# Key, value and gate products of two batches as three fp32r products each, with the norm's affine folded into the weights

## The chip, the cores and the metric

The kernel runs on 1 core of one Trainium2 chip. The metric is device microseconds of one execution, and the number quoted for a kernel is the median of its runs. TensorE is PE, its weight loads PEld, VectorE DVE, ScalarE ACT, GpSimd POOL and SyncE SP.

## The reference, cut to what matters

Four batches (B=4) of T=1024 tokens with D=128 features go through two time-mixing layers, a layer norm, a mixture of eight experts (top 2, hidden width 512) and a last norm. One time-mixing layer is

```python
normed = _layer_norm(x, ln_w, ln_b)            # (x - mu) * rsqrt(var + EPS) * w + b
k = einsum('btd,ed->bte', normed, Wk)
v = einsum('btd,ed->bte', normed, Wv)
r = sigmoid(einsum('btd,ed->bte', normed, Wr))
state = 0.95 * state + 0.05 * (k * v)           # a scan over the tokens
y = einsum('btd,ed->bte', r * state, Wo);  return x + y
```

and an expert computes `silu((x Wfc + bfc) * (x Wgate + bgate)) Wproj + bproj`.

## The kernel before

**Order of the work.** A head does the time mixing of batches 0 and 1 and the routing of batch 0. Then come four periods, one for each batch b, in which the experts of batch b run. A period has 32 points (8 experts times 4 blocks of 128 hidden units). Beside the experts of batch b, period b also routes batch b+1 and mixes batch b+2; the batches 2 and 3 are therefore mixed inside the periods 0 and 1. The order of each engine is written out by hand in tables that say what follows which point: TENSOR_MIX, SCALAR_MIX, VECTOR_MIX and POOL_MIX for the mixing of batch b+2 (lines 106 to 135). Every engine works through its own list in order and waits on semaphores.

**A point.** PE multiplies the gathered tokens by a gate block and an fc block (`hidden_pair`, lines 760 to 780): each is three fp32r matmuls of 308 columns, high part by high part, low by high and high by low. ACT copies the gate product out and adds its bias (`gate_copy`, line 984, tile gate_s), DVE multiplies (`product`, line 1299, tile prod), ACT takes silu of two blocks at a time (`silu`, line 991, tile hidden), PE projects (`project`, line 795) after the points 2 and 3 of the next expert, and DVE copies the result out (`copy_out`, line 1311) at the first point of an expert. `hidden_pair` of a point waits for the product of two points before.

**Mixing of batch 2 or 3.** It goes by halves of 512 tokens, n = 0 and 1 for the first layer, n = 2 and 3 for the second. For one half: DVE norms (`norm_of`, line 1095; it waits for POOL's rstd), PE transposes the four tiles into bank[0] (`turn`, line 619, after points 9, 12, 18 and 21), ACT copies bank[0] out with ln_w as scale and ln_b as bias (`turned`, line 912, tile normT), and PE multiplies (`kvr`, lines 639, 649 and 651, after points 10, 13, 20 and 22): k into bank[1], v into bank[2], r into bank[0], each one fp32 matmul of 512 columns, which the records show as two. ACT copies k (`k_of`, line 929) and takes tanh of r (`r_of`, line 939). DVE multiplies k and v (line 1112), scans (1122) and forms r times the state (1127): `mix`, after points 11, 14, 21 and 23. PE multiplies by Wo (`out`, line 679), DVE adds to x (line 1147) and takes the statistics of the next norm (lines 1070 and 1076).

**DVE's list around the halves** (VECTOR_MIX): norm(1) stands after the product of point 9, norm(3) after that of point 19, mix(0), mix(1), mix(2), mix(3) after those of 11, 14, 21 and 23. The copy_out of an expert stands ahead of the products of points 12, 20 and 24, skip_sum (line 1103) after that of point 20.

**Head.** Its lists are TENSOR_HEAD to POOL_HEAD (lines 67 to 99). The last entries of DVE are stats(2,0), stats(2,1) and slots(0,0) to slots(0,2); the last three form the low parts of the first gathered tokens (line 1161), for which the first expert waits.

Of the kernel before, what the change touches and what calls it, by code (L numbers as in the profile page):

```python
# [36 lines left out]
P = 128  # L37
# [32 lines left out]
               ("logits", 0, 0), ("logits", 0, 1), ("turn", 1, 0), ("turn", 1, 1), ("count", 0, 0),  # L70
               ("kvr", 1, 0), ("kvr", 1, 1), ("carry", 1, 0), ("out", 1, 0), ("carry", 1, 1), ("out", 1, 1),
               ("turn", 1, 2), ("turn", 1, 3), ("kvr", 1, 2), ("kvr", 1, 3), ("carry", 1, 2), ("out", 1, 2),
# [19 lines left out]
               ("scan", 1, 3), ("low", 6, 0), ("low", 6, 1), ("stats", 1, 4), ("stats", 1, 5), ("low", 7, 0),  # L92
               ("low", 7, 1), ("stats", 2, 0), ("stats", 2, 1), ("slots", 0, 0), ("slots", 0, 1),
               ("slots", 0, 2)]
# [17 lines left out]
SCALAR_ROUTE = {2: [("turned", 4)], 4: [("turned", 5)], 6: [("lead", 0)]}  # L112
VECTOR_MIX = {6: [("norm", 0)], 9: [("norm", 1)], 11: [("mix", 0)], 14: [("mix", 1)], 15: [("add", 0), ("stats", 2)],
              16: [("norm", 2)], 17: [("add", 1)], 18: [("stats", 3)], 19: [("norm", 3)], 20: [("skip_sum", 0)],
              21: [("mix", 2)], 23: [("mix", 3)], 24: [("add", 2)], 25: [("stats", 4)], 27: [("add", 3)],
              28: [("stats", 5)]}
# [89 lines left out]
def time_mix_moe(nc, h, ln_w, ln_b, Wk, Wv, Wr, Wo, router_w, router_b, w_fc, b_fc, w_gate, b_gate,  # L206
                 w_proj, b_proj, out):
    with ExitStack() as ctx:
        def sb(name, shape, dt=F32):
            return ctx.enter_context(nc.sbuf_tensor(name, shape, dt))  # L210
# [377 lines left out]
        def _(pe):  # L588
# [33 lines left out]
            def kvr(b, n):  # L622
                half = slice(HALF * (n % 2), HALF * (n % 2) + HALF)
                layer = n // 2
                c = step(b, n)
                between = banks_between(b)
                ps_r, ps_k, ps_v = mix_banks(b, n)
                if c > between:
                    pe.wait_ge(k_copied, c - between)
                fill("kvr", b, n, ps_k)  # L630
                if c == 1:
                    pe.wait_ge(weights_copied, 2)
                pe.wait_ge(turned_sb[0], c)
# [11 lines left out]
                if n == 2 and b >= 2:  # L645
                    pe.wait_ge(x_added, step(b, 1))
                if n == 0 and b >= 2:
                    pe.wait_ge(logits_copied, nth(b - 1, 2, 2))
                nc.tensor.matmul(ps_v[:, :], w_mix[:, L + layer, :], normT[:, half], start=True, stop=True)\  # L649
                  .then_inc(v_made, 1)  # L650
                nc.tensor.matmul(ps_r[:, :], w_mix[:, 2 * L + layer, :], normT[:, half], start=True, stop=True)\  # L651
                  .then_inc(r_made, 1)

            def carry(b, n):
# [73 lines left out]

            stages = {"turn": turn, "kvr": kvr, "out": out, "logits": logits, "count": count, "carry": carry}

# [29 lines left out]
            def hidden_pair(b, e, j):  # L760

                c = e * HC + j
                cols = slice(e * SLOTS, e * SLOTS + COLS)
                chunk = slice(P * j, P * j + P)
                if j == 0:
                    pe.wait_ge(slots_copied, nth(b, GROUPS, (e * SLOTS + COLS - 1) // (4 * P) + 1))
                if c == 0 and not later(b):
                    for read in (r_copied, k_copied, kv_made):
                        pe.wait_ge(read, nth(1, 4, 4))
                    pe.wait_ge(rows_made, 1)  # L770
                    pe.wait_ge(pool_low_made, 2 * LOW_BY_POOL)
# [124 lines left out]
        def _(act):  # L896
            def turned(b, n):
# [12 lines left out]
                tokens = slice(HALF * half, HALF * half + HALF)  # L910
                if not last:
                    nc.scalar.activation(normT[:, tokens], mix_banks(b, n)[0][:, :], ACT.Identity,
# [7 lines left out]
            def k_of(b, n):  # L920
# [6 lines left out]
                if c > 2 and n % 2 == 0:  # L927
                    act.wait_ge(state_made, c - 1)
                nc.scalar.activation(kv_sb[:, half], mix_banks(b, n)[1][:, :], ACT.Copy, scale=(1.0 - DECAY) / 2)\
                  .then_inc(k_copied, 1)  # L930

            def r_of(b, n):
# [4 lines left out]
                if c > 2:  # L937
                    act.wait_ge(out_made, c - 2)
                nc.scalar.activation(mixed[:, half], mix_banks(b, n)[0][:, :], ACT.Tanh, scale=0.5)\
                  .then_inc(r_copied, 1)  # L940

# [45 lines left out]
            def silu(b, e, i):  # L987
                act.wait_ge(prod_made, nth(b, POINTS, e * HC + 2 * i + 2))
                if e >= 2 or later(b):
                    act.wait_ge(o_made, nth(b, E, e - 1))  # L990
                nc.scalar.activation(hidden[:, e % 2, 2 * i:2 * i + 2, 0:COLS], prod[:, e % 2, 2 * i:2 * i + 2, :],  # L991
                                     ACT.Silu).then_inc(hidden_made, 1)

# [58 lines left out]
        def _(dve):  # L1052
# [53 lines left out]
            def kv_of(b, n):  # L1106
# [103 lines left out]
            def rows(b, _):  # L1210
# [28 lines left out]
                if b == LAST:  # L1239
# [4 lines left out]
            stages = {"stats": stats_of, "norm": norm_of, "kv": kv_of, "scan": scan_of, "mix": mix, "skip_sum": skip_sum, "add": add, "top": top,  # L1244
                      "choice": choice, "rows": rows, "slots": slots_low, "low": low_of}

# [46 lines left out]
            def product(b, e, j):  # L1293
# [3 lines left out]
                if j == 0 and (e >= 2 or later(b)):  # L1297
                    dve.wait_ge(hidden_made, nth(b, 2 * E, 2 * e - 2))
                nc.vector.scalar_tensor_tensor(prod[:, e % 2, j, :], pair[c % 2][1][:, 0:COLS], bfc_sb[:, e, j:j + 1],  # L1299
                                               gate_s[:, c % 2, :], ALU.add, ALU.mult).then_inc(prod_made, 1)  # L1300
# [361 lines left out]
```

## Time and profile before

| what | value |
|---|---|
| median of 3 runs | 366.13 us |
| lowest, highest run | 363.21 us, 367.05 us |
| span of the profiled execution, first to last instruction | 382.6 us |
| PE busy | 332.7 us, 87% of the span |
| DVE busy | 262.8 us, 69% |
| ACT, POOL busy | 166.2 us (43%), 203.9 us (53%) |

For the profiled execution the page gives the span and no other time of its own; what lies around the span is not stated. It is 16.5 us longer than the median of the runs. A matmul's record lasts longer than its turn on the engine, because matmuls are pipelined: what it costs PE is the distance from its start to the start of the next. The same holds, by less, for DVE and ACT. In the views PE's chain of waits is given in turns and the timeline in records.

### The profile page before, as it was taken

Reading aid. Unit: us, or ns where it says so; the run is one execution under the profiler, and the core shown is the slowest. Engines: PE = TensorE matmul, PEld = TensorE weight load, DVE = VectorE, ACT = ScalarE, POOL = GpSimd, SP = SyncE. Lnnn points to the kernel's source line nnn. Section 1 sums busy time; section 2 is a strip of 40 time slices with the busy share of each in tenths; the row PEclk is TensorE's granted clock in tenths of the full one; section 3 lists DMA queues with packets and bytes.
Section 4 is the critical chain, followed back from the end, with each engine's and each line's share of the span. In section 5 each row is a group of like instructions: output and inputs, shape, how many; then the busy total and the mean of one; then the engine's idle time right before and its main releaser. Section 6 shows DMA issues by size and latency. Waiting matters only on the chain.

```text
span 382.6 us, 7195 instructions
## 1 busy us (share of the span) xinstructions
PE 332.7 (87%) x2338; PEld 292.0 (76%) x2338; DVE 262.8 (69%) x853; ACT 166.2 (43%) x302; POOL 203.9 (53%) x244
## 2 busy tenths in 40 slices
PE   6889975869999999999999999877799986997880
PEld 3555653669879789997888999877689886987870
DVE  6688895787668868787787798831437684675225
ACT  2644434436545445555454445432435443363200
POOL 4185078850345642244557668377554437764752
PEclk9999896969999999999999999996999999898996
DMA  8949743150131133111114532222256111111152
GB/s 207 207 58 203 186 147 119 59 140 2 32 100 36 50 87 99 35 48 33 38 37 174 150 100 54 61 75 62 61 138 121 37 42 51 23 47 40 28 153 69
DMA packets 61246, 32.61 MB, mean 85 GB/s; under 512 B 15995, under 2 KB 58823, under 8 KB 61210
## 3 DMA queue, kind: packets, MB, share of 16 engines
q1 hardware_dynamic: 55322, 23.43, 25.3%
q0 software_dynamic: 4256, 7.94, 7.2%
q10 hardware_dynamic: 1632, 0.79, 0.7%
q8 instruction: 19, 0.31, 0.3%
q14 instruction: 17, 0.14, 0.1%
HBM read 19.01 MB, written 13.69 MB: 85 GB/s over the span
## 4 chain that ended last, share of the span: by engine, by line
PE 67%; issue 9%; DVE 8%; POOL 7%; another core or an unknown queue 3%; DMA 3%; ACT 3%; POOLq 0%; DVEq 0%; ACTq 0%
PE ps_o L795 20%; POOL slot_rows L1495 3%; PE pair0g L780 3%; PE pair0g L778 3%; PE pair1g L778 3%; PE bank L756 3%; PE bank L639 2%; PE pair1g L780 2%; PE bank L649 2%; PE pair0g L779 2%; PE bank L619 2%; PE pair1g L779 2%; PE bank L651 2%; PE pair1h L778 2%
## 5 line engine op out<-in xcount | busy, mean ns | idle before, releaser
L795 PE MATMUL ps_o<-proj_sb,hidden 128*104 128x128 f32 x768 | 99.7, 279 | 4.2 <-DVE o_sb L1311 2.1
L795 PEld LDWEIGHTS ps_o<-proj_sb,hidden 128*104 128x104 f32 x768 | 93.3, 175 | 5.8 <-issue 5.4
L1495 POOL DMA_INDIRECT slot_rows<-x_rows,row_to x64 | 72.5, 1133 | 45.1 <-DVE prod L1299 25.8
L1547 POOL DMA_INDIRECT picked<-expert_rows,row_from x48 | 49.9, 1039 | 37.4 <-DVE prod L1299 24.3
L984 ACT ACTIVATE gate_s<-pair0g,bgate_sb 128x308 f32<-128x308 f32 x64 | 33.1, 517 | 81.8 <-PE pair0g L780 52.7
L1299 DVE SCALAR_TENSOR_TENSOR prod<-pair1h,bfc_sb,gate_s 128x308 f32<-128x308 f32 x64 | 34.0, 532 | 32.3 <-ACT gate_s L984 17.7
L1299 DVE SCALAR_TENSOR_TENSOR prod<-pair0h,bfc_sb,gate_s 128x308 f32<-128x308 f32 x64 | 34.2, 534 | 26.4 <-ACT gate_s L984 11.8
L991 ACT ACTIVATE hidden<-prod 128x616 f32<-128x616 f32 x64 | 45.6, 712 | 7.7 <-DVE prod L1299 7.7
L984 ACT ACTIVATE gate_s<-pair1g,bgate_sb 128x308 f32<-128x308 f32 x64 | 33.0, 515 | 33.8 <-PE pair1g L780 22.2
L778 PE MATMUL pair1g<-slotT_hi,gate_hi 128*128 128x308 f32 x64 | 26.6, 416 | 10.0 <-DVE prod L1299 4.9
L1512 POOL DMA_INDIRECT returned<-o_sb,home x21 | 21.6, 1029 | 17.3 <-DVE prod L1299 11.2
L778 PE MATMUL pair0g<-slotT_hi,gate_hi 128*128 128x308 f32 x64 | 26.2, 409 | 4.0 <-DVE prod L1299 3.9
L1471 POOL TENSOR_TENSOR rstd<-shifted,power 128x4 f32<-128x4 f32 x24 | 26.2, 1093 | 2.0
L1311 DVE TENSOR_TENSOR o_sb<-ps_o,bproj_sb 104x384 f32<-104x384 f32 x32 | 17.5, 547 | 11.7 <-PE ps_o L795 7.4
L778 PEld LDWEIGHTS pair1g<-slotT_hi,gate_hi 128*128 128x128 f32 x64 | 12.4, 194 | 13.5 <-DVE prod L1299 6.7
L1467 POOL TENSOR_SCALAR shifted<-moments 128x4 f32<-128x4 f32 x24 | 6.8, 283 | 29.3 <-DVE moments L1076 29.1
L1161 DVE TENSOR_TENSOR slotT_lo<-bank,slotT_hi 128x512 fp32r<-128x512 f32 x20 | 13.8, 690 | 9.8 <-ACT slotT_hi L968 9.7
L1122 DVE TENSOR_TENSOR_SCAN kv_sb<-decay,kv_sb 128x512 f32<-128x512 f32 x16 | 20.1, 1255 | 0.6
L778 PE MATMUL pair0h<-slotT_hi,fc_hi 128*128 128x308 f32 x64 | 20.0, 312 | 0.0
L780 PE MATMUL pair0h<-slotT_hi,fc_lo 128*128 128x308 f32 x64 | 19.9, 312 | 0.0
L780 PE MATMUL pair0g<-slotT_hi,gate_lo 128*128 128x308 f32 x64 | 19.9, 311 | 0.0
L779 PE MATMUL pair0h<-slotT_lo,fc_hi 128*128 128x308 f32 x64 | 19.9, 311 | 0.0
(233 smaller groups left out, 773.0 us busy)
## 6 DMA issues: line engine op xcount, KB each, us to landing
slot_in<-slot_rows SPq DMA_DIRECT2D x20, 260.0 KB
expert_rows<-o_sb SPq DMA_DIRECT2D x24, 156.0 KB
x_in<-in_L_attn_h SPq DMA_DIRECT2D x4, 512.0 KB, 5.7
x_rows<-in_L_ffn_w_gate SPq DMA_DIRECT2D x8, 256.0 KB
x_rows<-in_L_ffn_w_c_fc SPq DMA_DIRECT2D x8, 256.0 KB
proj_sb<-in_L_ffn_w_c_proj SPq DMA_DIRECT2D x8, 256.0 KB, 5.3
out<-picked SPq DMA_DIRECT2D x12, 128.0 KB, 2.6
slot_rows<-slot_in SPq DMA_DIRECT2D x5, 260.0 KB, 7.2
```

What stands on the lines that cost most here:

```text
L778: nc.tensor.matmul(ps, hi[:, e, chunk], slotT_hi[:, cols], start=True, stop=False)
L779: nc.tensor.matmul(ps, hi[:, e, chunk], slotT_lo[:, cols], start=False, stop=False)
L780: nc.tensor.matmul(ps, lo[:, e, chunk], slotT_hi[:, cols], start=False, stop=True).then_inc(made, 1)
L795: mm = nc.tensor.matmul(ps_o[0:PART, P * part:P * part + P], hidden[:, e % 2, c, PART * part:PART * part + PART], proj_sb[:, e, c, :], sta ...
L984: nc.scalar.activation(gate_s[:, c % 2, :], pair[c % 2][0][:, 0:COLS], ACT.Identity, bias=bgate_sb[:, e, j:j + 1]).then_inc(g_copied, 1)
L991: nc.scalar.activation(hidden[:, e % 2, 2 * i:2 * i + 2, 0:COLS], prod[:, e % 2, 2 * i:2 * i + 2, :], ACT.Silu).then_inc(hidden_made, 1)
L1122: nc.vector.tensor_tensor_scan(kv_sb[:, lo:hi], decay[:, :], kv_sb[:, lo:hi], kv_sb[:, lo - 1:lo] if n % 2 else 0.0, ALU.mult, ALU.add)\
L1299: nc.vector.scalar_tensor_tensor(prod[:, e % 2, j, :], pair[c % 2][1][:, 0:COLS], bfc_sb[:, e, j:j + 1], gate_s[:, c % 2, :], ALU.add, ALU ...
L1471: nc.gpsimd.tensor_tensor(rstd[:, r, norm, tiles], shifted[:, r, norm, tiles], power[:, 0:HT], ALU.pow)\
L1495: nc.gpsimd.indirect_dma_start(out=slot_rows, out_offset=bass.IndirectOffsetOnAxis(ap=row_to[:, c:c + 1], axis=0), in_=x_rows[:, b, c // K ...
L1512: nc.gpsimd.indirect_dma_start(out=returned, out_offset=bass.IndirectOffsetOnAxis(ap=home[:, PARTS * e + i:PARTS * e + i + 1], axis=0), in ...
L1547: nc.gpsimd.indirect_dma_start(out=picked[:, j, k, :], out_offset=None, in_=expert_rows[b % 2], in_offset=bass.IndirectOffsetOnAxis(ap=row ...
```

## The change

For batches 2 and 3 `turned` no longer applies ln_w and ln_b. ACT copies bank[0] to half_hi (fp32r), DVE forms half_lo = bank[0] - half_hi (`turned_rest`, list name "rest"), and k, v and r are three fp32r matmuls each, against weights scaled_hi and scaled_lo that hold w_mix times ln_w in two parts. ln_b times the weights comes in as shift_mix, at ACT's copies of k and r (a bias operand) and at DVE's product of k and v. The weights and shift_mix are made once, in the head. Apart from that, `product` writes straight to hidden and silu works in place there, and prod is gone. Batches 0 and 1 stay as they were.

```diff
 TENSOR_HEAD: ("out", 1, 1), then
+              ("shift", 1, 0),
 SCALAR_HEAD: ("high", 5, 0), ("high", 5, 1), then
+              ("shift", 1, 0), ("scaled", 1, 0), ("scaled", 1, 1),
 VECTOR_HEAD: ("stats", 2, 0), ("stats", 2, 1), then
+              ("scaled", 1, 0), ("scaled", 1, 1),
-VECTOR_MIX = {6: [("norm", 0)], 9: [("norm", 1)], 11: [("mix", 0)], 14: [("mix", 1)], 15: [("add", 0), ("stats", 2)],
-              16: [("norm", 2)], 17: [("add", 1)], 18: [("stats", 3)], 19: [("norm", 3)], 20: [("skip_sum", 0)],
-              21: [("mix", 2)], 23: [("mix", 3)], ...
+VECTOR_MIX = {6: [("norm", 0)], 9: [("norm", 1), ("rest", 0)], 11: [("mix", 0)], 12: [("rest", 1)], 14: [("mix", 1)], 15: [("add", 0), ("stats", 2)],
+              16: [("norm", 2)], 17: [("add", 1)], 18: [("stats", 3)], 19: [("norm", 3), ("rest", 2)], 20: [("skip_sum", 0)],
+              21: [("mix", 2)], 22: [("rest", 3)], 23: [("mix", 3)], ...
+            def split_kvr(b, n, layer, c):
+                ps_r, ps_k, ps_v = mix_banks(b, n)
+                hi, lo = scaled_hi[:, layer, :, :], scaled_lo[:, layer, :, :]
+                nc.tensor.matmul(ps_k[:, :], hi[:, 0, :], half_hi[:, :], start=True, stop=False)
+                nc.tensor.matmul(ps_k[:, :], lo[:, 0, :], half_hi[:, :], start=False, stop=False)
+                pe.wait_ge(kv_made, c - banks_between(b))
...
+                nc.tensor.matmul(ps_v[:, :], hi[:, 1, :], half_hi[:, :], start=True, stop=False)
+                nc.tensor.matmul(ps_v[:, :], lo[:, 1, :], half_hi[:, :], start=False, stop=False)
+                pe.wait_ge(turned_low, nth(b - 2, 4, n + 1))
+                nc.tensor.matmul(ps_k[:, :], hi[:, 0, :], half_lo[:, :], start=False, stop=True).then_inc(k_made, 1)
+                nc.tensor.matmul(ps_v[:, :], hi[:, 1, :], half_lo[:, :], start=False, stop=True).then_inc(v_made, 1)
+                nc.tensor.matmul(ps_r[:, :], hi[:, 2, :], half_hi[:, :], start=True, stop=False)
+                nc.tensor.matmul(ps_r[:, :], lo[:, 2, :], half_hi[:, :], start=False, stop=False)
+                nc.tensor.matmul(ps_r[:, :], hi[:, 2, :], half_lo[:, :], start=False, stop=True).then_inc(r_made, 1)
+            def shift(_, n):                      # PE: six matmuls of one column
+                for w in range(3):
+                    for layer in range(L):
+                        i = L * w + layer
+                        mm = nc.tensor.matmul(pair[1][1][:, i:i + 1], w_mix[:, i, :], lnb_sb[:, layer:layer + 1], ...)
 turned (ACT), b >= 2:
+                    act.wait_ge(r_made, step(b, n) - 1)
+                    nc.scalar.activation(half_hi[:, :], mix_banks(b, n)[0][:, :], ACT.Copy).then_inc(turned_sb[0], 1)
 k_of (ACT), b >= 2:
+                    nc.scalar.activation(kv_sb[:, half], mix_banks(b, n)[1][:, :], ACT.Identity,
+                                         bias=shift_mix[:, n // 2:n // 2 + 1], scale=(1.0 - DECAY) / 2)
 r_of (ACT), b >= 2:
+                    nc.scalar.activation(mixed[:, half], mix_banks(b, n)[0][:, :], ACT.Tanh,
+                                         bias=shift_mix[:, 2 * L + n // 2:2 * L + n // 2 + 1], scale=0.5)
+            def shift(_, n):                      # ACT: three copies of two columns
+            def scaled(_, layer):                 # ACT: scaled_hi = w_mix * ln_w, 384 columns
+            def scaled_of(_, layer):              # DVE: scaled_lo = w_mix * ln_w - scaled_hi, 384 columns
 kv_of (DVE), b >= 2:
+                    nc.vector.scalar_tensor_tensor(kv_sb[:, lo:hi], mix_banks(b, n)[2][:, :],
+                                                   shift_mix[:, L + n // 2:L + n // 2 + 1], kv_sb[:, lo:hi], ALU.add, ALU.mult)
+            def turned_rest(b, n):                # DVE
+                dve.wait_ge(turned_sb[0], step(b, n))
+                dve.wait_ge(r_made, step(b, n) - 1)
+                nc.vector.tensor_tensor(half_lo[:, :], mix_banks(b, n)[0][:, :], half_hi[:, :].bitcast(F32), ALU.subtract)\
+                  .then_inc(turned_low, 1)
 silu (ACT):
-                if e >= 2 or later(b):
-                    act.wait_ge(o_made, nth(b, E, e - 1))
-                nc.scalar.activation(hidden[:, e % 2, 2 * i:2 * i + 2, 0:COLS], prod[:, e % 2, 2 * i:2 * i + 2, :], ACT.Silu)
+                both = hidden[:, e % 2, 2 * i:2 * i + 2, 0:COLS]
+                nc.scalar.activation(both, both, ACT.Silu).then_inc(hidden_made, 1)
 product (DVE):
-                    dve.wait_ge(hidden_made, nth(b, 2 * E, 2 * e - 2))
-                nc.vector.scalar_tensor_tensor(prod[:, e % 2, j, :], ...)
+                    dve.wait_ge(o_made, nth(b, E, e - 1))
+                nc.vector.scalar_tensor_tensor(hidden[:, e % 2, j, 0:COLS], ...)
```

## Rows read from the trace of the kernel before

**Rows 1.** Busy time of the engines in periods 0 and 1 (PE, PEld, DVE, ACT, POOL, PEclk, DMA).

```profile
82.80:154.40 71.60, 70.79 (x514) 64.08 (x513) 55.03 (x174) 38.03 (x71) 26.52 (x31) 0.98 0.22 60
154.40:225.90 71.50, 70.59 (x525) 63.73 (x525) 56.13 (x175) 36.87 (x69) 38.35 (x41) 1.00 0.27 79
```

**Rows 2.** The chain that ended last, at the first kvr of batch 2: start, length.

```profile
101.87 0.86 PE bank L639 x2
```

**Rows 3.** Timeline of PE, period 0: start us, record us, instruction.

```profile
99.68 0.31 PE L779 MATMUL pair0g<-slotT_lo,gate_hi 128*128 128x308 f32 x1
...
100.39 1.47 PE L795 MATMUL ps_o<-proj_sb,hidden 128*104 128x128 f32 x12
...
104.42 0.30 PE L779 MATMUL pair1g<-slotT_lo,gate_hi 128*128 128x308 f32 x1
...
111.80 0.30 PE L779 MATMUL pair0g<-slotT_lo,gate_hi 128*128 128x308 f32 x1
...
128.42 0.31 PE L779 MATMUL pair1g<-slotT_lo,gate_hi 128*128 128x308 f32 x1
...
134.51 0.30 PE L779 MATMUL pair1g<-slotT_lo,gate_hi 128*128 128x308 f32 x1
...
139.85 0.41 PE L778 MATMUL pair0g<-slotT_hi,gate_hi 128*128 128x308 f32 x1 [0.55 <-DVE prod L1299]
```

**Rows 4.** Timeline of DVE, period 0.

```profile
101.83 0.53 DVE L1299 SCALAR_TENSOR_TENSOR prod<-pair0h,bfc_sb,gate_s 128x308 f32<-128x308 f32 x1
105.59 0.54 DVE L1299 SCALAR_TENSOR_TENSOR prod<-pair1h,bfc_sb,gate_s 128x308 f32<-128x308 f32 x1 [3.23 <-issue]
...
109.61 0.53 DVE L1299 SCALAR_TENSOR_TENSOR prod<-pair1h,bfc_sb,gate_s 128x308 f32<-128x308 f32 x1
...
126.43 1.11 DVE L1095 TENSOR_SCALAR normed<-x_mid,moments,rstd 128x128 f32<-128x128 f32 x4 [1.06 <-POOL rstd L1471]
127.46 0.55 DVE L1311 TENSOR_TENSOR o_sb<-ps_o,bproj_sb 104x384 f32<-104x384 f32 x1
...
129.59 0.54 DVE L1299 SCALAR_TENSOR_TENSOR prod<-pair1h,bfc_sb,gate_s 128x308 f32<-128x308 f32 x1
...
132.71 0.53 DVE L1299 SCALAR_TENSOR_TENSOR prod<-pair0h,bfc_sb,gate_s 128x308 f32<-128x308 f32 x1
...
139.26 0.53 DVE L1299 SCALAR_TENSOR_TENSOR prod<-pair0h,bfc_sb,gate_s 128x308 f32<-128x308 f32 x1
```

**Rows 5.** ACT's copies of 512 columns, grouped by line and shape: count, busy us, mean ns.

```profile
L912 ACT ACTIVATE normT<-bank,lnb_sb,lnw_sb 128x512 f32<-128x512 f32 x12 | 9.3, 777 | 9.8 <-PE bank L619 6.2 <-issue 3.6
...
L929 ACT ACTIVATE kv_sb<-bank 128x512 f32<-128x512 f32 x12 | 7.2, 597 | 7.1 <-PE bank L639 6.8
```

**Rows 6.** Timeline of PE, period 1.

```profile
175.93 0.31 PE L779 MATMUL pair1g<-slotT_lo,gate_hi 128*128 128x308 f32 x1
...
183.31 0.30 PE L779 MATMUL pair0g<-slotT_lo,gate_hi 128*128 128x308 f32 x1
...
199.93 0.31 PE L779 MATMUL pair1g<-slotT_lo,gate_hi 128*128 128x308 f32 x1
```

**Rows 7.** Timeline of DVE, period 1.

```profile
173.89 0.53 DVE L1299 SCALAR_TENSOR_TENSOR prod<-pair0h,bfc_sb,gate_s 128x308 f32<-128x308 f32 x1
...
181.65 0.53 DVE L1299 SCALAR_TENSOR_TENSOR prod<-pair1h,bfc_sb,gate_s 128x308 f32<-128x308 f32 x1
...
199.49 0.55 DVE L1311 TENSOR_TENSOR o_sb<-ps_o,bproj_sb 104x384 f32<-104x384 f32 x1
```

**Rows 8.** Timeline of the head's end: DVE's first low part.

```profile
81.60 0.69 DVE L1161 TENSOR_TENSOR slotT_lo<-bank,slotT_hi 128x512 fp32r<-128x512 f32 x1 [0.29 <-ACT slotT_hi L968]
```

**Rows 9.** The chain that ended last, in period 3.

```profile
322.00 2.87 issue
324.87 0.62 PE pair1g L778
325.50 0.26 PE pair1g L779
```

More of the change, by code:

```diff
@@ L70 @@
                ("logits", 0, 0), ("logits", 0, 1), ("turn", 1, 0), ("turn", 1, 1), ("count", 0, 0),
-               ("kvr", 1, 0), ("kvr", 1, 1), ("carry", 1, 0), ("out", 1, 0), ("carry", 1, 1), ("out", 1, 1),
+               ("kvr", 1, 0), ("kvr", 1, 1), ("carry", 1, 0), ("out", 1, 0), ("carry", 1, 1), ("out", 1, 1), ("shift", 1, 0),
                ("turn", 1, 2), ("turn", 1, 3), ("kvr", 1, 2), ("kvr", 1, 3), ("carry", 1, 2), ("out", 1, 2),
@@ L92 @@
                ("scan", 1, 3), ("low", 6, 0), ("low", 6, 1), ("stats", 1, 4), ("stats", 1, 5), ("low", 7, 0),
-               ("low", 7, 1), ("stats", 2, 0), ("stats", 2, 1), ("slots", 0, 0), ("slots", 0, 1),
+               ("low", 7, 1), ("stats", 2, 0), ("stats", 2, 1), ("scaled", 1, 0), ("scaled", 1, 1), ("slots", 0, 0), ("slots", 0, 1),
                ("slots", 0, 2)]
@@ L245, in time_mix_moe @@
         normT = sb("normT", [P, T])
+        half_hi = sb("half_hi", [P, HALF], F32R)
+        half_lo = sb("half_lo", [P, HALF], F32R)
         kv_sb = sb("kv_sb", [P, T])
@@ L349, in time_mix_moe @@
         weights_copied = sem("weights_copied")
+        shift_made = sem("shift_made")
+        shift_copied = sem("shift_copied")
+        scaled_high = sem("scaled_high")
+        scaled_made = sem("scaled_made")
+        turned_low = sem("turned_low")
         stats_made = [sem("stats_made"), sem("stats_made_last")]
@@ L638, in kvr @@
                     pe.wait_ge(slots_copied, nth(b - 2, GROUPS, 5))
+                if b >= 2:
+                    return split_kvr(b, n, layer, c)
                 nc.tensor.matmul(ps_k[:, :], w_mix[:, layer, :], normT[:, half], start=True, stop=True)\
@@ L727, in count @@
                 mm.then_inc(counts_made, 1)
-            stages = {"turn": turn, "kvr": kvr, "out": out, "logits": logits, "count": count, "carry": carry}
+            stages = {"turn": turn, "kvr": kvr, "out": out, "logits": logits, "count": count, "carry": carry, "shift": shift}
             def turn_slots(b, g):
@@ L773, in hidden_pair @@
                     pe.wait_ge(x_added, step(1, 3))
+                    pe.wait_ge(shift_copied, 3)
                 if c >= 2 or later(b):
@@ L910, in turned @@
                 tokens = slice(HALF * half, HALF * half + HALF)
-                if not last:
+                if not last and b >= 2:
+                    act.wait_ge(r_made, step(b, n) - 1)
+                    nc.scalar.activation(half_hi[:, :], mix_banks(b, n)[0][:, :], ACT.Copy)\
+                      .then_inc(turned_sb[0], 1)
+                elif not last:
                     nc.scalar.activation(normT[:, tokens], mix_banks(b, n)[0][:, :], ACT.Identity,
@@ L928, in k_of @@
                     act.wait_ge(state_made, c - 1)
-                nc.scalar.activation(kv_sb[:, half], mix_banks(b, n)[1][:, :], ACT.Copy, scale=(1.0 - DECAY) / 2)\
-                  .then_inc(k_copied, 1)
+                if b < 2:
+                    nc.scalar.activation(kv_sb[:, half], mix_banks(b, n)[1][:, :], ACT.Copy, scale=(1.0 - DECAY) / 2)\
+                      .then_inc(k_copied, 1)
+                else:
+                    nc.scalar.activation(kv_sb[:, half], mix_banks(b, n)[1][:, :], ACT.Identity,
+                                         bias=shift_mix[:, n // 2:n // 2 + 1], scale=(1.0 - DECAY) / 2)\
+                      .then_inc(k_copied, 1)
             def r_of(b, n):
@@ L938, in r_of @@
                     act.wait_ge(out_made, c - 2)
-                nc.scalar.activation(mixed[:, half], mix_banks(b, n)[0][:, :], ACT.Tanh, scale=0.5)\
-                  .then_inc(r_copied, 1)
+                if b < 2:
+                    nc.scalar.activation(mixed[:, half], mix_banks(b, n)[0][:, :], ACT.Tanh, scale=0.5)\
+                      .then_inc(r_copied, 1)
+                else:
+                    nc.scalar.activation(mixed[:, half], mix_banks(b, n)[0][:, :], ACT.Tanh,
+                                         bias=shift_mix[:, 2 * L + n // 2:2 * L + n // 2 + 1], scale=0.5)\
+                      .then_inc(r_copied, 1)
+            def shift(_, n):
+                act.wait_ge(shift_made, 1)
+                for w, by in enumerate(((1.0 - DECAY) / 2, 1.0, 0.5)):
+                    nc.scalar.activation(shift_mix[:, L * w:L * w + L], pair[1][1][:, L * w:L * w + L], ACT.Copy, scale=by)\
+                      .then_inc(shift_copied, 1)
+            def scaled(_, layer):
+                nc.scalar.activation(scaled_hi[:, layer, :, :],
+                                     w_mix[:, 0:3 * L, :].rearrange("p (w l) d -> p w l d", l=L)[:, :, layer, :],
+                                     ACT.Copy, scale=lnw_sb[:, layer:layer + 1]).then_inc(scaled_high, 1)
             def kr(b, n):
@@ L1244, in _ @@
             stages = {"stats": stats_of, "norm": norm_of, "kv": kv_of, "scan": scan_of, "mix": mix, "skip_sum": skip_sum, "add": add, "top": top,
-                      "choice": choice, "rows": rows, "slots": slots_low, "low": low_of}
+                      "choice": choice, "rows": rows, "slots": slots_low, "low": low_of, "scaled": scaled_of,
+                      "rest": turned_rest}
             def first_sum(b, q):
```

45 lines of the change are left out of this document (33 added, 12 removed).

## The prediction

> **What bounds the kernel now.** I read the busy time by stage first: in periods 0 and 1, where batches 2 and 3 are mixed, PE is busy 70.8 of 71.6 us and 70.6 of 71.5 us, DVE 55.0 and 56.1 us, at a granted clock of 0.98 and 1.00 [rows 1]. So a shorter PE would shorten these stages. The chain that ended last says the same: at kvr it runs along PE itself, 0.86 us for one fp32 product of 512 columns [rows 2]. Then I read the timelines of PE and DVE side by side around the four places of kvr, since the change puts a new DVE instruction between PE's transpose and the end of kvr. There the reader is to see how late DVE is: it does the norm of the half (second of a layer) and the products of the points well after PE has passed them [rows 4, 7].
>
> **What PE saves.** Before, a kvr is 3 x 0.86 = 2.58 us [rows 2]. Now it is nine fp32r matmuls of 512 columns. The trace has fp32r at 308 columns only: five turns from 99.68 to 100.39, 0.142 us each [rows 3]. Lower bound for 512: a quarter of the fp32 product, 0.215 us; upper bound: 0.142 x 512/308 = 0.236 us. I take 0.228, which is 0.142 plus 204 columns at the fp32 rate per pass (0.86/2048 = 0.00042 us each). Nine are 2.05 us: 0.53 us saved in a half, in 8 halves 4.2 us, if PE never waits. The first four (k and v by the high half) are 0.91 us, the last five 1.14 us.
> The Trainium skill, "TensorE: Matmul & The Clock Gate" (Back-to-back issue gap), gives N/2.4 GHz plus 2.5 ns. For 308 columns that would be 131 ns, where the row has 142; for 512 it would be 216 ns and a saving of 0.64 us a half, which moves the sum below by about 0.5 us.
>
> **What DVE adds.** One subtraction from PSUM of 512 columns in each of 8 halves; the same form takes 0.69 us at L1161 [rows 8]. PE sees it some 0.06 us later, as after DVE's product at 139.26 (0.53 us long) PE starts at 139.85 [rows 3, 4]: landing = start + 0.75. The wait for it (turned_low) stands after the first four matmuls, and behind it on PE are five matmuls of kvr and then the expert's matmuls, which are the critical work. So wherever DVE is late, kvr ends at landing + 1.14, however fast its matmuls are.
>
> **What ACT does.** Its copy of bank[0] loses two per-partition operands: 0.78 to 0.60 us [rows 5]. k and r gain one each, about 0.09 us. r's copy is ahead of the next gate_copy, on which DVE's next product hangs: DVE's work after a kvr moves with the end of kvr, plus 0.09. Bounds of that are 0 and 0.18.
>
> **Place by place, period 0.** PE's end of kvr is the start of the L779 that follows, less one turn of 0.142.
> - kvr(0): before 101.70 to 104.28 [rows 3]. rest(0) starts when norm(1) is done, at 101.83, where product(10) stood [rows 4], and lands at 102.58; PE is at the wait at 102.61. No wait; end 103.75, 0.53 early.
> - kvr(1): before it ends at 111.66. DVE moves by -0.53 + 0.09 = -0.44. rest(1) stands where the product of point 13 began, 109.61 [rows 4]; now 109.17, landing 109.92, end 111.06: 0.60 early.
> - kvr(2): before 125.70 to 128.28. rest(2) comes behind norm(3), which itself idles 1.06 us for POOL's rstd, and ahead of the copy_out at 127.46 [rows 4]. Moved by -0.51: start 126.95, landing 127.70, while PE is at the wait at 126.0. PE idles 1.7 us; end 128.84, 0.56 late.
> - kvr(3): from the end of a kvr to the next product on DVE are 1.31 us (104.28 to 105.59), now 1.40; mix(2) puts product(22) 3.12 us behind product(21) (129.59 to 132.71) [rows 4]; rest(3) follows 0.45 to 0.53 later, 0.45 taken. Landing is 128.84 + 1.40 + 3.12 + 0.45 + 0.75 = 134.56, end 135.70, against 134.37 before: 1.33 late. Between the ends of kvr(2) and kvr(3) 0.77 us are lost.
> With ACT's 0.09, PE's next wait for DVE (139.85 [rows 3]) moves 1.4 us. Period 0: +1.4.
>
> **Period 1**, by its own rows. DVE is later there. kvr(0): rest at 173.89 [rows 7], landing 174.64, end 175.78, before 175.79 [rows 6]: nothing won. kvr(1): rest at 181.65 + 0.08, end 183.62, before 183.17: +0.45. kvr(2): rest at 199.49 + 0.54, landing 200.78, end 201.92, before 199.79: +2.13, with PE idle for 2.2 us. kvr(3): +0.77 as above. Period 1: +2.9, with ACT's 0.09 +3.0.
>
> **The rest.** Head: PE's six one-column products and ACT's five small operations stand ahead of turn(1,2), in a stretch where both wait for DVE's norms; taken at nothing, and without that cover under 2 us. DVE's two low parts of the weights (384 columns, about 0.6 us each) stand straight ahead of slots(0,0), which begins at 81.60 and on which the first expert waits; DVE has 0.29 us of idle there [rows 8]. Bounds 0 and 0.9 us, taken 0.3. Silu in place: the product now waits for a projection that PE's order puts ahead of that product's own matmuls, and the sizes are unchanged; nothing. DVE's product of k and v takes one more operand; nothing.
>
> **Sum.** 1.4 + 3.0 + 0.3 = +4.7 us. Against the profiled execution: 382.6 to 387.3 us of span. The page gives no time beside the span; the runs are 16.5 us below it, and nothing in the sum hangs on that difference, so for the median: 366.1 + 4.7 = 370.8 us. With 0.215 us a matmul, a shorter hand-over and a free head it is +3.4, with 0.236 and the head at 0.9 it is +5.6: own range 368.5 to 372.5.
>
> **Rivals.**
> - *PE's saving arrives.* If DVE's subtraction is never late, 8 x 0.53 less the head's 0.3 gives -3.9: 362.2 us. For it: PE is 99% busy in both periods [rows 1]. Against it: the subtraction must start at least 1.7 and 2.2 us earlier at kvr(2), and DVE's norm just ahead of it is finished no earlier [rows 4, 7]. Chance 0.14.
> - *Only kvr(2) waits.* DVE's lag at the other places may be smaller in the runs than in this profile. Then six halves save 3.2, the two kvr(2) lose 0.56 + 0.53 and 2.13 - 0.45, 2.8 together, and the head 0.3: 366 us, no change. Chance 0.16.
> - *The clock falls in the waits.* Slower than the forecast too. After 2.87 us of idle at 322.00 PE's turns are 0.26 in place of 0.14 us [rows 9], which is 1.2 GHz for 2.4, for some 3.4 us: 1.7 us lost each time. My longest waits, 1.7 and 2.2 us, come near. Once or twice: +6.4 to +8.1, 372.5 to 374.2, taken 373.5. It decides if PE idles over 2 us at once. Against it: idles of 0.55 us leave the clock alone [rows 1, 3]. Chance 0.15. The Trainium skill's page on TensorE ("HAM oscillation — how this bites in real kernels") says that idle gaps between bursts put the clock back to half; the rows agree for the long gap.
> - The forecast: 0.55.
>
> **How the numbers follow.** About 1% (3.7 us) is what a measurement of this kernel tells from no change. Faster: most of the first rival, 0.12. Same: the second, the rest of the first, and a third of the forecast (ends under 369.8), 0.34. Slower: 0.54. The range goes from 363 to 375 us; it leaves out half of the first rival and the end of the third.
>
> **What would show it.** kvr's first four matmuls 0.22 to 0.24 us apart; on PE idle ahead of the fifth, released by DVE half_lo, none at the first kvr of batch 2, about 0.7 to 1.3 us at the other kvr(0), kvr(1) and kvr(3), and 1.7 and 2.2 us at kvr(2); PE busy less, both periods longer (73.0 and 74.5 us for 71.6 and 71.5). I am wrong if PE passes the fifth matmul without idle, if both periods are shorter, or if periods 2 and 3 change by more than the early ones.

## The result, and the profile after

The changed kernel takes 370.82 us (median of 5 runs, 370.74 to 372.78) against 366.13 us before (363.21 to 367.05); the ratio is 1.0171, 95% interval 1.0124 to 1.0219. Run again on another chip (4 runs, 370.90 to 374.33) beside 20 runs of the kernel before, it took 372.08 us against 365.42 us, ratio 1.0206 (1.0171 to 1.0241). The ratios are worked out from the fast runs alone and are not the quotients of the medians given (those are 1.013 and 1.018 here). The kernel is slower: by 4.7 and 6.7 us as the medians have it, by 6.3 and 7.5 us as the ratios have it, where the forecast had 4.7. Both intervals exclude no change; whether the loss is over or under 2% they leave open.

The busy times of the engines over the whole span of the changed kernel, from its page:

```profile
span 371.0 us, 7235 instructions
...
PE 327.6 (88%) x2374; PEld 293.0 (79%) x2374; DVE 268.9 (72%) x863; ACT 167.3 (45%) x307; POOL 202.3 (55%) x244
```

Neither the 327.6 us for 332.7 on PE nor the 371.0 us for 382.6 us of span can be read as an effect of the change. The difference lies in the periods 2 and 3, where the change touches nothing (the kernel before, then the changed one, columns as in rows 1):

```profile
225.76:382.60 156.84, 127.60 (x969) 121.58 (x967) 87.86 (x279) 57.43 (x108) 91.72 (x107) 0.93 0.26 66
232.97:371.00 138.03, 120.93 (x969) 117.10 (x967) 87.60 (x279) 57.19 (x108) 91.47 (x107) 0.96 0.29 75
```

For the same 969 matmul records the profile before has 6.7 us more of busy time, at a granted clock of 0.93 for 0.96, and 12 us more of idle (2.87 us of it stands in rows 9). In all other profiles of this study these two periods take 136 to 139 us. So the periods 0 and 1 are compared.

The changed kernel's two periods by engine (their limits rounded, where PE turns to the next batch's experts; same columns as rows 1):

```profile
83.40:156.80 73.40, 69.47 (x525) 65.15 (x526) 57.70 (x178) 38.11 (x71) 25.60 (x31) 0.99 0.22 57
156.80:233.10 76.30, 71.27 (x538) 66.84 (x537) 58.91 (x179) 36.96 (x69) 38.25 (x41) 0.98 0.27 74
```

They answer to [rows 1]: PE was busy 70.8 of 71.6 and 70.6 of 71.5 us, and is now busy 69.5 of 73.4 and 71.3 of 76.3 us. Idle on PE rose from 1 to 4 and 5 us. That PE's busy time did not fall in period 1 comes from a lower clock there, shown below. Whom PE waits for, in the changed kernel's list of waits (us in total, times, longest):

```profile
PE bank L676 <- DVE half_lo L1201: 7.1, 7, 1.9
```

L676 is the fifth matmul of kvr, the first one that reads half_lo; L1201 is the new subtraction. PE waits for it at seven of the eight halves. The second layer's first half, kvr(2), in period 0 (timeline of PE and DVE: start us, record us, instruction):

```profile
126.63 0.40 PE L674 MATMUL bank<-half_hi,scaled_lo 128*128 128x512 f32 x1
126.67 1.11 DVE L1164 TENSOR_SCALAR normed<-x_mid,moments,rstd 128x128 f32<-128x128 f32 x4 [1.06 <-POOL rstd L1561]
127.70 0.68 DVE L1201 TENSOR_TENSOR half_lo<-bank,half_hi 128x512 fp32r<-128x512 f32 x1
128.44 0.50 PE L676 MATMUL bank<-half_lo,scaled_hi 128*128 128x512 f32 x1 [1.41 <-DVE half_lo L1201]
128.78 0.39 PE L678 MATMUL bank<-half_lo,scaled_hi 128*128 128x512 f32 x1
...
129.47 0.39 PE L682 MATMUL bank<-half_lo,scaled_hi 128*128 128x512 f32 x1
```

The reader is to see DVE idle for 1.06 us ahead of its norm, the norm, and only then the subtraction, while PE has nothing to do from about 126.9 (the fourth matmul's start plus a turn of 0.23 us; the view counts the idle from the end of its record, 0.17 us later). The first turn after the wait is 0.34 us (128.44 to 128.78), not 0.23; it is 0.33 to 0.34 behind each of the other waits for half_lo at full clock. The same place in period 1:

```profile
201.22 0.40 PE L674 MATMUL bank<-half_hi,scaled_lo 128*128 128x512 f32 x1
...
202.80 0.68 DVE L1201 TENSOR_TENSOR half_lo<-bank,half_hi 128x512 fp32r<-128x512 f32 x1
203.54 0.60 PE L676 MATMUL bank<-half_lo,scaled_hi 128*128 128x512 f32 x1 [1.92 <-DVE half_lo L1201]
...
204.36 0.63 PE L680 MATMUL bank<-half_hi,scaled_hi 128*128 128x512 f32 x1
204.79 0.63 PE L681 MATMUL bank<-half_hi,scaled_lo 128*128 128x512 f32 x1
205.22 0.63 PE L682 MATMUL bank<-half_lo,scaled_hi 128*128 128x512 f32 x1
```

Here the turns after the wait are 0.43 us, where they are 0.23 at the other halves. The granted clock of the stretch that follows (columns as in rows 1; the clock is the last but two):

```profile
203.50:208.00 4.50, 4.46 (x18) 3.94 (x19) 2.63 (x5) 2.07 (x4) 3.53 (x3) 0.62 0.75 265
```

The granted clock is 0.62 over these 4.5 us: some three quarters of it were spent at 1.2 GHz, the rest at 2.4, after PE had idled 1.92 us.

### The profile page after: what moved, and what is told of

Same layout as the page of the kernel before. It is cut to its first block, busy times and chain, and to the rows that moved or that the text cites. A ratio compares the mean times of both kernels' runs of the same rounds, so it can differ in the third digit from the quotient of the medians.

```text
span 371.0 us, 7235 instructions
## 1 busy us (share of the span) xinstructions
PE 327.6 (88%) x2374; PEld 293.0 (79%) x2374; DVE 268.9 (72%) x863; ACT 167.3 (45%) x307; POOL 202.3 (55%) x244
## 4 chain that ended last, share of the span: by engine, by line
PE 51%; DVE 17%; issue 11%; POOL 10%; DMA 6%; ACT 3%; DVEq 0%; POOLq 0%; SPq 0%; ACTq 0%
PE ps_o L838 14%; POOL slot_rows L1585 4%; DVE kv_sb L1211 3%; DVE hidden L1389 3%; PE bank L798 2%; PE ps_o L602 2%; PE pair0g L821 2%; PE pair1g L821 2%; DMA slot_in<-slot_rows 2%; POOL rstd L1561 2%; PE pair0g L823 1%; PE pair0g L822 1%; DMA picked<-expert_rows,row_from 1%; PE pair1g L823 1%; DVE kv_sb L1185 1%
## 5 line engine op out<-in xcount | busy, mean ns | idle before, releaser
L1585 POOL DMA_INDIRECT slot_rows<-x_rows,row_to x64 | 71.0, 1109 | 47.4 <-DVE hidden L1389 29.0
L838 PE MATMUL ps_o<-proj_sb,hidden 128*104 128x128 f32 x768 | 96.2, 273 | 0.3 <-DVE o_sb L1401 0.2
L838 PEld LDWEIGHTS ps_o<-proj_sb,hidden 128*104 128x104 f32 x768 | 90.1, 170 | 1.2 <-issue 0.7
L1055 ACT ACTIVATE gate_s<-pair0g,bgate_sb 128x308 f32<-128x308 f32 x64 | 33.1, 517 | 71.6 <-PE pair0g L823 71.6
L1389 DVE SCALAR_TENSOR_TENSOR hidden<-pair1h,bfc_sb,gate_s 128x308 f32<-128x308 f32 x64 | 33.9, 530 | 24.9 <-ACT gate_s L1055 22.8
L1061 ACT ACTIVATE hidden<-hidden 128x616 f32<-128x616 f32 x64 | 45.5, 711 | 10.2 <-DVE hidden L1389 10.2
L1389 DVE SCALAR_TENSOR_TENSOR hidden<-pair0h,bfc_sb,gate_s 128x308 f32<-128x308 f32 x64 | 34.0, 531 | 14.8 <-ACT gate_s L1055 14.1
L821 PE MATMUL pair1g<-slotT_hi,gate_hi 128*128 128x308 f32 x64 | 23.7, 370 | 3.9 <-DVE hidden L1389 3.8
L823 PE MATMUL pair1g<-slotT_hi,gate_lo 128*128 128x308 f32 x64 | 19.6, 307 | 0.0
L822 PE MATMUL pair1h<-slotT_lo,fc_hi 128*128 128x308 f32 x64 | 19.6, 307 | 0.0
L821 PE MATMUL pair1h<-slotT_hi,fc_hi 128*128 128x308 f32 x64 | 19.6, 306 | 0.0
```

The source lines that it names most:

```text
L838: mm = nc.tensor.matmul(ps_o[0:PART, P * part:P * part + P], hidden[:, e % 2, c, PART * part:PART * part + PART], proj_sb[:, e, c, :], sta ...
L1055: nc.scalar.activation(gate_s[:, c % 2, :], pair[c % 2][0][:, 0:COLS], ACT.Identity, bias=bgate_sb[:, e, j:j + 1]).then_inc(g_copied, 1)
L1061: nc.scalar.activation(both, both, ACT.Silu).then_inc(hidden_made, 1)
L1389: nc.vector.scalar_tensor_tensor(hidden[:, e % 2, j, 0:COLS], pair[c % 2][1][:, 0:COLS], bfc_sb[:, e, j:j + 1], gate_s[:, c % 2, :], ALU.a ...
L1585: nc.gpsimd.indirect_dma_start(out=slot_rows, out_offset=bass.IndirectOffsetOnAxis(ap=row_to[:, c:c + 1], axis=0), in_=x_rows[:, b, c // K ...
```

## The experiments

Lengths of period 0 and of period 1 are used below: period 0 from PE's first gate matmul of batch 0 to the projection of 24 records that opens the next batch, period 1 from there to the same projection of the batch after (19 to 22 of its records are kept in some profiles). Runs of e1 to e4 were on one chip, e5 to e8 on a second and e9 to e12 on a third, each group beside its own runs of the kernel before (medians 365.70, 365.42 and 364.82 us), so medians of two groups are compared with that in mind.

### e1: no low part of the tokens

```diff
-VECTOR_MIX: ("rest", 0), ("rest", 1), ("rest", 2), ("rest", 3)
-                pe.wait_ge(turned_low, nth(b - 2, 4, n + 1))
-                nc.tensor.matmul(ps_k[:, :], hi[:, 0, :], half_lo[:, :], ...)
+                nc.tensor.matmul(ps_k[:, :], hi[:, 0, :], half_hi[:, :], ...)   # so for v and r
```

> The changed kernel without half_lo: no subtraction on DVE and no wait for it; kvr keeps its nine fp32r matmuls, and those that read half_lo read half_hi. It leaves out the low part of the tokens. Late-subtraction theory: all that was lost came by the wait, so kvr now takes 9 x 0.23 = 2.1 us for 2.58 in all eight halves; that is 4 us saved against the kernel before, less 0.3 to 0.6 in the head: about 362.5 us (ratio 0.990). Rival, that the loss comes from PE's nine matmuls or from the dearer copies of ACT: no faster than the kernel before, 366 us or more. Rival, that it comes from the head or silu in place: also 366 or more.

Measured: 361.16 us (360.21 to 361.69), before 365.70, ratio 0.990 (0.9855 to 0.9944). The kernel leaves out the low part of the tokens and takes the high part twice, so its k, v and r are not those of the reference; it only serves to find the cause. The nine matmuls, ACT's copies with their new operand and the head all together leave a gain of 4.5 us or so: the whole of the loss, and the loss of the gain, hangs on the subtraction and its wait.

### e4: the subtraction's time alone

```diff
 (kernel before, with silu in place)
+            def turned_rest(b, n):        # at the places of the change in VECTOR_MIX
+                dve.wait_ge(turned_sb[0], step(b, n))
...
+                nc.vector.tensor_tensor(idle_lo[:, :], decay[:, :], idle_in[:, :], ALU.subtract)
```

> The kernel before, silu in place, with a subtraction of 512 columns of the same length on DVE at the four places of the change in both periods, for whose result nobody waits; kvr is the old one with fp32 matmuls and waits for ACT alone. Late-subtraction theory: DVE's time alone costs little, since PE is the bound: 0 to +1.5 us over the kernel before (DVE's products of points 12, 20 and 24 move by up to 0.6 us, and PE waits for the one of point 24). Rival, that DVE's extra time is what costs: +4 to +5 us as in the changed kernel.

Measured: 364.02 us (361.95 to 365.12), ratio 0.9976 (0.9944 to 1.0009): no difference. Its subtractions take 0.68 us, as those of the change do, and stand in the same places; they read SBUF tiles in place of the PSUM bank. DVE's time costs nothing that these runs can tell by itself, though it pushes DVE's later products back by 0.6 us a half; that PE waits for the result is what costs.

### e2: one subtraction ahead of the norm

```diff
-19: [("norm", 3), ("rest", 2)]
+19: [("rest", 2), ("norm", 3)]
```

> The changed kernel with one swap in DVE's list: at point 19 the subtraction rest(2) stands ahead of norm(3) instead of behind it, where DVE idled 1.06 us for POOL. Late-subtraction theory: the wait at kvr(2) (1.4 and 1.9 us in the trace of the changed kernel, and five matmuls plus an expert point at half clock after the second, some 1.5 us) goes, the other waits stay: 370.8 - 3.3 to - 4.8 = 366.0 to 367.5 us. Rival, that DVE's extra 0.6 us a half costs by itself wherever it stands: within 0.5 us of the changed kernel, 370.3 to 371.

Measured: 369.29 us (367.93 to 369.96), ratio 1.0131 (1.0085 to 1.0177). That is 1.5 us under the 370.8 of the changed kernel's first runs and 2.8 under its second, less than the 3.3 to 4.8 expected. The wait at kvr(2) is gone, but part of it came back one half later (timeline of e2, the first of each pair in period 0, the second in period 1):

```profile
124.40 0.39 PE L666 MATMUL bank<-half_hi,scaled_hi 128*128 128x512 f32 x1
...
125.33 0.40 PE L676 MATMUL bank<-half_lo,scaled_hi 128*128 128x512 f32 x1
...
132.60 0.50 PE L676 MATMUL bank<-half_lo,scaled_hi 128*128 128x512 f32 x1 [1.41 <-DVE half_lo L1201]
```

```profile
206.37 0.50 PE L676 MATMUL bank<-half_lo,scaled_hi 128*128 128x512 f32 x1 [1.91 <-DVE half_lo L1201]
```

At kvr(3) PE waited 1.05 and 0.86 us in the changed kernel and waits 1.41 and 1.91 us here: DVE reaches rest(3) by its own pace, and PE arrives earlier. My expectation had kept these waits as they were. In this profile, of the fastest of the six runs (367.93 us), the clock did not fall after the 1.91 us either (columns as in rows 1), and the periods are 72.2 and 73.8 us, together 3.7 to 3.9 less than in the two profiles of the changed kernel:

```profile
206.50:208.00 1.50, 1.50 (x8) 1.28 (x9) 0.00 (x0) 0.00 (x0) 0.97 (x1) 1.00 0.00 0
```

### e10: only the last subtraction earlier

```diff
-21: [("mix", 2)], 22: [("rest", 3)]
+21: [("kv", 2), ("rest", 3), ("scan", 2)]
```

> The changed kernel with only rest(3) earlier, between the product of k and v and the scan of half 2; rest(0) to rest(2) stay. Late-subtraction theory: the waits of 1.05 and 0.86 us at kvr(3) go (1.9 us), those at kvr(0) to kvr(2) and the fall of the clock stay: 1.5 to 2 us under the changed kernel, 370 to 370.5 beside 372. From the run with rest(2) alone (waits at kvr(3) grew to 1.41 and 1.91 us) it follows that rest(2) and rest(3) together are worth more than the sum of each: kvr(3) waits for work of DVE that PE's own wait at kvr(2) had put off.

Measured: 367.99 us (365.66 to 371.64), ratio 1.0094 (1.0051 to 1.0137), some 2 us better than expected. The waits at kvr(3) are gone as expected and those at kvr(2) are there in full; but the clock did not fall this time (columns as in rows 1):

```profile
201.86 0.50 PE L676 MATMUL bank<-half_lo,scaled_hi 128*128 128x512 f32 x1 [1.92 <-DVE half_lo L1201]
202.90 0.39 PE L682 MATMUL bank<-half_lo,scaled_hi 128*128 128x512 f32 x1
```

```profile
200.00:205.00 5.00, 3.14 (x19) 2.75 (x20) 4.23 (x10) 2.03 (x4) 3.89 (x5) 1.00 0.41 130
```

After the same 1.92 us of idle the clock stays at 1.00. Its period 1 is 73.8 us, 2.3 to 2.5 less than in the two profiles of the changed kernel. The twelve runs lie 6 us apart, and for eleven of them no profile says whether the clock held, so why the median is under the expectation stays open.

### e3 and e11: all four subtractions earlier

```diff
-9: [("norm", 1), ("rest", 0)], 11: [("mix", 0)], 12: [("rest", 1)], ... 19: [("norm", 3), ("rest", 2)]
-21: [("mix", 2)], 22: [("rest", 3)]
+9: [("rest", 0), ("norm", 1)], 11: [("mix", 0), ("rest", 1)], ... 19: [("rest", 2), ("norm", 3)]
+21: [("kv", 2), ("rest", 3), ("scan", 2)]
```

> The changed kernel with all four subtractions earlier in DVE's list: rest(0) ahead of norm(1), rest(1) straight behind mix(0), rest(2) ahead of norm(3), rest(3) between the product of k and v and the scan of half 2. Nothing else differs. Late-subtraction theory: at all eight places the subtraction lands before PE has done the first four matmuls, or within 0.3 us of it, so the saving on PE arrives nearly whole: 362.5 to 364 us, below the kernel before. Rival, that DVE's extra time costs by itself: 370 us.

> The kernel of e3 once more, beside e12 on one chip: 361.5 to 362.5 us.

Measured: 361.94 us (360.25 to 365.25), ratio 0.9915 (0.9878 to 0.9952), and 361.17 us (359.38 to 363.53), ratio 0.9897 (0.9849 to 0.9945). Nothing but DVE's order differs from the changed kernel, and 9 to 11 us lie between the medians; in the traces the periods 0 and 1 take 139.8 and 140.0 us together, where the changed kernel has 149.8 and 149.6. This version leaves nothing out and beats both kernels, by 3.7 to 3.8 us the kernel before. In the list of waits of its periods 0 and 1 PE no longer waits for half_lo; at kvr(2) of period 0 (timeline):

```profile
124.28 0.68 DVE L1201 TENSOR_TENSOR half_lo<-bank,half_hi 128x512 fp32r<-128x512 f32 x1
124.68 0.39 PE L666 MATMUL bank<-half_hi,scaled_hi 128*128 128x512 f32 x1
...
125.42 1.11 DVE L1164 TENSOR_SCALAR normed<-x_mid,moments,rstd 128x128 f32<-128x128 f32 x4 [0.46 <-POOL rstd L1561]
125.61 0.40 PE L676 MATMUL bank<-half_lo,scaled_hi 128*128 128x512 f32 x1
...
126.55 0.39 PE L682 MATMUL bank<-half_lo,scaled_hi 128*128 128x512 f32 x1
```

The subtraction fills DVE's idle of 1.06 us (0.46 are left), the norm is no later for it, and the nine turns take 2.1 us without a gap.

### e5, e6, e8 and e12: the head and silu

e5 keeps of the change only the head's work and silu in place:

> The changed kernel with the mixing of batches 2 and 3 as before (fp32 kvr, norm weight and bias in ACT's copy, no subtraction): of the change only the weights in two parts and the shift, made in the head, and silu in place remain. My ledger had 0.3 us for the head (bounds 0 and 0.9) and nothing for silu: 366 to 366.6 us. The rival that the head carries the loss: over 369.

Measured: 363.78 us (363.14 to 365.79), before 365.42, ratio 0.9968 (0.9949 to 0.9987). e6 is the kernel before with silu in place alone:

> The kernel before with one edit: the product writes to hidden and silu works in place. Prediction of the ledger: no difference, within 0.3% of the kernel before. Rival, that reading and writing one tile or the moved waits cost something: over 1% slower.

Measured: 364.48 us (363.22 to 366.36), ratio 0.9987 (0.9967 to 1.0007). Neither costs anything that can be told. The 0.3 us of the ledger for the head does not show; e5 is even a little under the kernel before, for which I have no cause. e8 and e12 move DVE's two low parts of the weights in e3's kernel to an earlier idle:

```diff
-("stats", 1, 4), ("stats", 1, 5), ... ("stats", 2, 1), ("scaled", 1, 0), ("scaled", 1, 1), ("slots", 0, 0)
+("stats", 1, 4), ("scaled", 1, 0), ("scaled", 1, 1), ("stats", 1, 5), ... ("stats", 2, 1), ("slots", 0, 0)
```

> The kernel of e3 (all four subtractions early) with DVE's two low parts of the weights moved from the end of the head to between stats(1,4) and stats(1,5), where DVE idled 0.84 us for PE in e3. If the end of the head hangs on DVE's list, slots(0,0) begins up to 1.0 us earlier and 0.3 to 0.8 us are won over e3's 361.9; if it hangs on the scattered tokens' load instead, nothing.

> The kernel of e8 once more, beside e11 on one chip. If DVE's two low parts of the weights at the end of the head cost what stands before slots(0,0) there (1.0 us less the 0.3 us of idle), it is 0.3 to 0.8 us under e11; if the first experts hang on the load of the scattered tokens, it is the same.

Measured: 361.17 us (360.22 to 364.03, ratio 0.9899), and beside e11 362.24 us (359.94 to 364.34, ratio 0.9921) against e11's 361.17. No gain: the first expert hangs on something other than these 1.0 us, or the gain is below what the runs tell. The start of PE's first gate matmul lies anywhere between 81.4 and 83.2 us in the fourteen profiles of this study, with and without the head's work.

### e7 and e9: the clock

> The changed kernel once more, to see whether TensorE's clock falls at kvr(2) of batch 3 in every execution. In the first profile it did, after 1.9 us of idle, and that execution took 372.8 us where the others took 370.7 to 371.1. If the fall is what sets it apart, a profile without it has five matmuls of 0.23 us after that wait and period 1 is some 1.5 us shorter than in the first profile (74.8 for 76.3 us); if it falls each time, the period is 76.3 us again.

Measured: 372.08 us (370.90 to 374.33), ratio 1.0206. The clock fell again, two matmuls later than in the first profile, and in this profile's own execution of 370.9 us; so the fall does not set apart the longer executions, as I had thought:

```profile
202.54 0.50 PE L676 MATMUL bank<-half_lo,scaled_hi 128*128 128x512 f32 x1 [1.93 <-DVE half_lo L1201]
202.87 0.40 PE L678 MATMUL bank<-half_lo,scaled_hi 128*128 128x512 f32 x1
203.11 0.59 PE L680 MATMUL bank<-half_hi,scaled_hi 128*128 128x512 f32 x1
203.50 0.63 PE L681 MATMUL bank<-half_hi,scaled_lo 128*128 128x512 f32 x1
```

Its period 1 is 76.1 us, as against 76.3.

```diff
+                if n == 2 and b == LAST:
+                    for _ in range(7):
+                        nc.tensor.matmul(ps_v[:, :]..., ones[:, :], ones..., start=True, stop=True)
                 nc.tensor.matmul(ps_v[:, :], hi[:, 1, :], half_hi[:, :], start=True, stop=False)
```

> The changed kernel with seven bf16 matmuls of 512 columns (0.21 us each, 1.5 us in all, result overwritten) at kvr(2) of batch 3, ahead of its first v product, so that PE computes through most of the 1.9 us in which it waits for half_lo. The wait ends at the same time. If the clock fell because PE idled there, it stays at 2.4 GHz: the last matmuls of kvr(2) are 0.23 us apart for 0.43, the expert's 0.145 for 0.26, period 1 goes from 76.1-76.3 us to 74.5-75.0 and the whole gains 1.2 to 1.7 us (about 370.5 beside a changed kernel of 372). If the clock has nothing to do with it: no difference.

Measured: 371.91 us (369.12 to 372.37), ratio 1.0183 (1.0137 to 1.0228); the gain of 1.2 to 1.7 us that I expected is not in the median. In its profile the clock stays: the wait left is 0.39 us and the turns after it 0.23.

```profile
203.67 0.50 PE L681 MATMUL bank<-half_lo,scaled_hi 128*128 128x512 f32 x1 [0.39 <-DVE half_lo L1206]
204.00 0.39 PE L683 MATMUL bank<-half_lo,scaled_hi 128*128 128x512 f32 x1
...
204.70 0.39 PE L687 MATMUL bank<-half_lo,scaled_hi 128*128 128x512 f32 x1
```

Period 1 is 75.1 us, 1.0 to 1.2 less than in the two profiles of the changed kernel. The medians do not resolve it: 0.2 us between them, on two chips, and intervals that overlap. From the end of kvr(1) to that of kvr(3) period 1 takes 25.51 us here, 26.71 and 26.43 us in the two profiles of the changed kernel: 0.9 to 1.2 us for the fall. That is less than the turns at half clock lose, since PE then comes later to kvr(3) and waits less there (0.86 and 0.57 us, here 1.05). This rests on one profile against two. That PE's idle is the cause of the fall is likely, but with e10 and e2, where as much idle left the clock alone, it was not settled.

## Why the prediction was right

**The mechanism** was as forecast: PE was the bound, its saving was there to be had, and the subtraction, placed behind DVE's norm and products, was late for it. e1 shows that without the wait the saving arrives, e3 that the place of the subtraction alone makes the wait, e4 that DVE's time is not it.

**PE's saving.** Forecast 0.228 us a matmul from the rows at 308 columns [rows 3]; the trace has 0.23 to 0.235 (126.63 back to 125.94 in three turns, and e3's 125.61 to 126.55 in four). The formula of the Trainium skill ("TensorE: Matmul & The Clock Gate", Back-to-back issue gap) would have had 0.216; for 512 columns of fp32r, each with its own weights, the row was the better guide. What the forecast lacks is the first turn after a wait: behind a landing the five matmuls took 1.26 to 1.28 us (128.44 to 129.70 at this one) where it had 1.14, at all six halves with a wait and full clock.

**The ends of kvr**, in distances from one end to the next, so that the head drops out (us; the fourth is the sum of the three):

| | kvr(0) to (1) | (1) to (2) | (2) to (3) | sum |
|---|---|---|---|---|
| period 0, before | 7.38 | 16.62 | 6.09 | 30.09 |
| forecast | 7.31 | 17.78 | 6.86 | 31.95 |
| measured | 7.48 | 18.03 | 7.02 | 32.53 |
| period 1, before | 7.38 | 16.62 | 6.09 | 30.09 |
| forecast | 7.84 | 18.30 | 6.86 | 33.00 |
| measured | 8.02 | 19.33 | 7.38 | 34.73 |
| measured in e9, clock held | 8.01 | 18.48 | 7.03 | 33.52 |

An end is the start of the last matmul plus its turn: 103.96, 111.44, 129.47, 136.49 and 0.23 in period 0, 178.07, 186.09, 205.22 (plus 0.43) and 212.80 in period 1. Each step of period 0 is within 0.25 us, and longer than forecast; half or more of that is the 0.12 us behind each landing. With the clock held the steps of period 1 are over by 0.17 to 0.18 us as well. PE's waits for half_lo: forecast none at the first, 0.7 to 1.3 us at the other kvr(0), kvr(1) and kvr(3), 1.7 and 2.2 us at kvr(2); the views have 0, 0.51, 1.41, 1.05 and 0.32, 1.04, 1.92, 0.86, and 0.17 us more for each of the seven waits if they are counted in turns as the forecast's were. The 0.5 us of kvr(0) in period 1 lies under the forecast's list, though its own working (wait reached at 174.12, landing at 174.64) gives just that.

**The terms.** Period 0: +1.4 forecast, 73.5 for 71.8 us, +1.7 measured (both profiles of the changed kernel). The start of the period hides part of it. The first 4 us of period 0, in the kernel before, the changed one and e6 (columns as in rows 1):

```profile
82.46:86.46 4.00, 4.00 (x20) 4.00 (x19) 3.45 (x9) 1.86 (x4) 0.45 (x1) 0.62 0.51 127
83.17:87.17 4.00, 4.00 (x24) 3.60 (x24) 3.50 (x10) 2.31 (x5) 0.24 (x1) 0.86 0.40 96
82.72:86.72 4.00, 4.00 (x25) 3.61 (x24) 3.52 (x10) 2.32 (x5) 0.00 (x0) 0.86 0.39 94
```

The profile before was at half clock for most of them (0.62). Against e6, the kernel before but for silu, which starts at the same clock as the changed one (0.86) and has 71.3 us, period 0 is +2.2; the steps between the ends of kvr have +2.4 us, of which the first kvr's saving of some 0.4 goes off. Period 1: +3.0 forecast, 76.1 to 76.3 for 71.5, +4.6 to +4.8 measured. This is the term that was mis-sized most: I had treated the fall of the clock as a rival in place of the forecast, with 0.15, and it came on top of it, in both profiles and at the place with the longest wait; with the clock held (e9) the period is +3.6. Head: +0.3 forecast, nothing measurable (e5). DVE's product of k and v with its new operand, put at nothing: 0.74 us for 0.68, and e3 gains all the same. Sum of the measured terms: +6.3 to +6.5, or +6.8 to +7.0 against e6's periods, where the two comparisons have +4.7 and +6.7 by their medians. That the first median is the forecast to the digit is luck: the kernel before had there, in its three runs shown and in all five of that comparison, a median 0.4 to 1.3 us over what the larger sets gave (365.70, 365.42 and 364.82).

**The rivals.** The saving would have arrived, about in the size of the 3.9 us forecast for it, had the subtraction not been late: 3.8 and 3.7 us under their own runs of the kernel before in e3 and e11, 4.5 in e1. The forecast held against this rival that DVE's norm is finished no earlier; the way out was to put the subtraction ahead of the norm. *The clock falls in the waits*, with its chance of 0.15, is what the two traces show, once in each: it had +6.4 us for one fall, from 1.7 us a fall and the rest as in the forecast, and the traces have +6.3 to +6.5, from 0.9 to 1.2 us for the fall, 0.3 and 0.6 us by which the two periods are longer than forecast without it, and nothing for the head. So the median agrees with the forecast, and the traces agree better with this rival. "Only kvr(2) waits" fell: PE waits at seven of eight.

**Silu in place**: nothing forecast, nothing measured (e6).

## What to carry to other kernels

Where a change splits one PE operation into parts that wait for different engines, read at each place when the slower engine gets to its new instruction: the engine's spare share of time (DVE had 23% and 21%) says nothing about that. Place the new instruction in the slower engine's list where its input is ready and the next thing waits anyway; here four moved entries of a table turned 1.7 to 2.1% of loss into 1% of gain. Repair all such places at once before judging: with one of them repaired, PE arrives earlier at the next and waits there.

## What the runs showed of the hardware that I had not expected

The granted clock fell after 1.92 and 1.93 us of idle on PE (0.62 over the 4.5 us from 203.5), and stayed at 1.00 after 1.92 us at the same place in e10 and after 1.91 us at kvr(3) in e2. Idle of this length is no safe ground in either direction. In [rows 9] it was 2.87 us, and I had taken 2 us as the point from which it decides; the runs show no such point.
An ACT copy of 512 columns with one per-partition operand took 0.69 us, between the 0.60 without and the 0.78 with two [rows 5].
